# Attention turns: next rows' halves scaled by GpSimd and VectorE, one each, low parts behind; first exponential in front of the rows' high parts

## The reference

```python
gamma = (t @ gamma_w.T)[:, None, :]
beta = (t @ beta_w.T)[:, None, :]
return gamma * _rmsnorm(x) + beta
```

## Time and profile before

| | us |
|---|---|
| median of 3 runs | 1043.72 |
| lowest, highest | 1042.64, 1046.42 |
| profiled execution, its own time | 1053.19 |
| its span in the profile | 1051.4 |
| TensorE busy | 1021.5 (97%) |
| VectorE busy | 762.1 (72%) |
| ScalarE busy | 627.5 (60%) |
| GpSimd busy | 223.2 (21%) |

### The profile page before, as it was taken

How to read it: one execution, slowest core, us unless ns; L and a number is a source line. 1 busy time by engine, 2 the same in 40 slices (tenths; PEclk the granted TensorE clock), 3 DMA queues, 4 the chain that set the end, 5 groups by cost and what they waited for, 6 DMA issues and landing times.

```text
span 1051.4 us, 16503 instructions
## 1 busy us (share of the span) xinstructions
PE 1021.5 (97%) x5386; PEld 639.3 (61%) x5386; DVE 762.1 (72%) x1200; ACT 627.5 (60%) x850; POOL 223.2 (21%) x217
## 2 busy tenths in 40 slices
PE   7999999999999999999999999999999999999997
PEld 6776677778554344444444344443368788888885
DVE  5867668887767778778777877778955766667754
ACT  5455333352247777778777877777763545555455
POOL 1000001121122324333432333311202221212211
PEclk9999999999699999999999999999999999999999
DMA  9978644125424363553537354454220000000001
GB/s 288 379 189 241 160 109 115 31 41 151 104 63 154 79 192 68 165 124 104 149 77 207 73 163 101 133 137 105 72 61 21 1 21 21 20 20 0 21 21 41
DMA packets 92041, 110.95 MB, mean 106 GB/s; under 512 B 47184, under 2 KB 57424, under 8 KB 90960
## 3 DMA queue, kind: packets, MB, share of 16 engines
q1 hardware_dynamic: 60736, 100.56, 32.6%
q10 hardware_dynamic: 31248, 9.65, 5.3%
HBM read 65.81 MB, written 33.03 MB: 94 GB/s over the span
## 4 chain that ended last, share of the span: by engine, by line
PE 70%; DVE 9%; ACT 4%; issue 4%; DMA 3%; SPq 1%; ACTq 1%; POOL 1%; DVEq 0%; POOLq 0%
PE st_ps L1787 16%; PE st_ps L1639 9%; PE mx_ps L1787 8%; PE av_ps L1616 7%; PE val_ps L1491 6%; PE gate_ps L1491 5%; DVE mx L1202 5%; PE misc_ps L1547 3%; PE misc_ps L1663 3%; PE mx_ps L1571 3%; PE misc_ps L1676 2%; PE y_ps L1501 2%; DMA hf<-reciprocals 2%; DVE stage L1214 1%; PE misc_ps L1667 1%
## 5 line engine op out<-in xcount | busy, mean ns | idle before, releaser
L1202 DVE TENSOR_REDUCE mx<-mx_ps 128x1 f32<-128x512 f32 x488 | 313.4, 683 | 100.1 <-PE mx_ps L1571 97.8
L1571 PE MATMUL mx_ps<-kring,qring 48*128 48x512 f32 x500 | 198.4, 462 | 2.4 <-DVE mx L1202 1.5
L1639 PE MATMUL st_ps<-qring,kring 50*128 50x512 f32 x512 | 187.0, 445 | 4.7 <-ACT shared L928 4.6
L1639 PEld LDWEIGHTS st_ps<-qring,kring 50*128 50x128 f32 x512 | 76.3, 185 | 148.2 <-issue 112.7
L928 ACT ACTIVATE pbuf<-st_ps 128x1024 f32<-128x1024 f32 x128 | 129.4, 1023 | 41.8 <-PE st_ps L1639 40.4
L928 ACT ACTIVATE shared<-st_ps 128x1024 f32<-128x1024 f32 x128 | 128.0, 1022 | 38.0 <-PE st_ps L1639 37.1
L1571 PEld LDWEIGHTS mx_ps<-kring,qring 48*128 48x128 f32 x500 | 85.4, 185 | 24.9 <-DVE mx L1202 19.1
L1049 ACT ACTIVATE p_hi<-shared 128x512 fp32r<-128x512 f32 x64 | 40.4, 632 | 90.8 <-DVE shared L1382 88.6
L1387 DVE TENSOR_TENSOR p_lo<-shared,p_hi 128x512 fp32r<-128x512 f32 x64 | 52.3, 817 | 46.9 <-ACT p_hi L1049 46.9
L1382 DVE TENSOR_TENSOR shared<-st_ps,shared 128x512 f32<-128x512 f32 x64 | 43.9, 687 | 51.6 <-PE st_ps L1787 24.2
L1268 DVE SCALAR_TENSOR_TENSOR h<-val_ps,r,gelu 128x1024 f32<-128x1024 f32 x32 | 41.0, 1282 | 47.9 <-PE val_ps L1491 47.9
(11 more groups left out here) (241 smaller groups left out, 2103.9 us busy)
## 6 DMA issues: line engine op xcount, KB each, us to landing
chunk<-in_gen_w SPq DMA_DIRECT2D x8, 2048.0 KB, 9.2
qring<-q_parts SPq DMA_DIRECT2D x64, 192.0 KB, 3.5
kring<-k_parts SPq DMA_DIRECT2D x64, 192.0 KB, 4.6
q_parts<-stage SPq DMA_DIRECT2D x16, 512.0 KB, 2.9
k_parts<-stage SPq DMA_DIRECT2D x16, 512.0 KB, 2.8
xres<-in_xT SPq DMA_DIRECT2D x8, 512.0 KB, 11.4
shared<-in_x SPq DMA_DIRECT2D x8, 512.0 KB, 12.5
q_parts<-stage SPq DMA_DIRECT2D x16, 256.0 KB, 3.0
```

Of the source, the lines that this page charges most:

```text
L1202: nc.vector.tensor_reduce(mx[h // GH % 2][:, col:col + 1], mx_ps[:, qt % 2], AX, ALU.max).then_inc(S["mx_free"], 1)
L1571: nc.tensor.matmul(out, qring[h // GH][r:r + QROWS, h % GH // 2, qt * P:(qt + 1) * P], kring[h // GH][r:r + QROWS, h % GH // 2, :], start= ...
L1639: ins = nc.tensor.matmul(st_ps[half][:, kt % 2], kring[g][r:r + SROWS, i % GH // 2, kt * P:(kt + 1) * P], qring[g][r:r + SROWS, i % GH // ...
```

## The change

Four edits, all in the attention turns:

1. ScalarE, i = 0 of turns 2 to 7: the first of the step's two exponentials stands in front of the two high parts, and the second behind them.
2. GpSimd, same place: scales half 0 of `hf` when the first high part is there. Then it makes both low parts; for half 0 it waits for its own scaling, for half 1 for VectorE's.
3. VectorE, same place: scales half 1 alone, and waits for both high parts and for GpSimd's scaling of half 0 (`h` counts the halves in order).
4. GpSimd's turns 3 to 6 are written out instead of looped.

```diff
@@ gpsimd, step @@
                     for k in range(KD):
-                        wait(pool, "h" if rows_by_two(j) else "h_hi", KD * p + k + 1)
+                        wait(pool, "h_hi", KD * p + k + 1)
+                        if rows_by_two(j) and k == 0:
+                            nc.gpsimd.tensor_scalar(hf[:, k], hf[:, k], cv[:, C_GA, k, bass.ds(p, 1)],
+                                                    cv[:, C_BA, k, bass.ds(p, 1)], ALU.mult, ALU.add) \
+                                .then_inc(S["h"], 1)
+                        if rows_by_two(j):
+                            wait(pool, "h", KD * p + k + 1)
                         sub(m_lo[:, k], hf[:, k], m_hi[:, k].bitcast(F32)).then_inc(S["h_lo"], 1)
...
-            for turn in iterations(pool):
+            for j in range(1, NB + 1):
                 for i in range(NH):
-                    step(*turn, i)
+                    step(*flags(j), i)
@@ scalar, step @@
-                if i == 0 and has_p and rows_by_two(j):
-                    for k in range(KD):
-                        wait(act, "t", KD * p + k + 1)
-                        nc.scalar.activation(m_hi[:, k], hf[:, k], ACT.Identity,
-                                             scale=cv[:, C_GA, k, bass.ds(p, 1)],
-                                             bias=cv[:, C_BA, k, bass.ds(p, 1)]).then_inc(S["h_hi"], 1)
-                elif i == 0 and has_p and not opens:
+                if i == 0 and has_p and not opens and not rows_by_two(j):
                     scale_rows()
...
                         nc.scalar.activation(pbuf[g % 2][:, i % GH, 2 * half:2 * half + 2], st_ps[half][:],
                                              ACT.Exp, scale=float(DH) ** -0.5).then_inc(S["exp"], 1)
+                        if half == 0 and i == 0 and has_p and rows_by_two(j):
+                            for k in range(KD):
+                                wait(act, "t", KD * p + k + 1)
+                                nc.scalar.activation(m_hi[:, k], hf[:, k], ACT.Identity,
+                                                     scale=cv[:, C_GA, k, bass.ds(p, 1)],
+                                                     bias=cv[:, C_BA, k, bass.ds(p, 1)]).then_inc(S["h_hi"], 1)
@@ vector, step @@
                 if i == 0 and has_p and rows_by_two(j):
-                    for k in range(KD):
-                        wait(dve, "h_hi", KD * p + k + 1)
-                        nc.vector.tensor_scalar(hf[:, k], hf[:, k], cv[:, C_GA, k, bass.ds(p, 1)],
-                                                cv[:, C_BA, k, bass.ds(p, 1)], ALU.mult, ALU.add) \
-                            .then_inc(S["h"], 1)
+                    wait(dve, "h_hi", KD * (p + 1))
+                    wait(dve, "h", KD * p + 1)
+                    nc.vector.tensor_scalar(hf[:, 1], hf[:, 1], cv[:, C_GA, 1, bass.ds(p, 1)],
+                                            cv[:, C_BA, 1, bass.ds(p, 1)], ALU.mult, ALU.add).then_inc(S["h"], 1)
```

## The result

| | before | changed |
|---|---|---|
| median, us (20 runs each, one chip) | 1045.24 | 1049.56 |
| lowest and highest, us | 1042.64, 1053.51 | 1047.22, 1054.77 |
| profiled execution: own time, span, us | 1053.19, 1051.4 | 1048.26, 1046.5 |
| its mean granted clock | 0.987 | 0.998 |

The ratio is 1.0036, with a 95% interval of 1.0022 to 1.0051: **3.8 us slower** (2.3 to 5.3), inside the 0.5% that was called no change, and measurably above zero. The two profiled executions stand the other way round, by 4.9 us, and the one of before has the lower clock. They are compared by seams, in stretches where the clock is 1.00 in both, and not by their spans.

What follows compares the result with a forecast made beforehand. TensorE bounds the kernel; the seam depends on the early exponential and, more strongly, VectorE's return to its maxima. Four seams losing 4.0 us and two gaining 0.7 give +3.3 on 1043.72: 1047.0 us, range 1041.8 to 1050.0.

Steps and rivals of the forecast that it cites:

- seams: The six passages between two attention turns, into turns 2 to 7; 3 to 6 looped, 2 and 7 written out.
- likeliest class: Whole kernel: a change of under 5.2 us (about 0.5%) either way, which counts as no change; chance 0.73.
- B: Rival: VectorE's scaling is held by GpSimd's subtraction in all six seams; +5.6 us, 1049.3; chance 0.10.
- the forecast, held in four: VectorE held in turns 3 to 6, 4.0 us lost; free in 2 and 7, 0.7 gained; +3.3; chance 0.55.
- Exponential first: Step 1's start: up to 0.43 us gained a seam, 2.6 over six, only if VectorE is not later.
- the 5.12: Turn 4's first query product, us from t = 0 (ScalarE starting the high parts), said to be set by VectorE's maxima.
- GpSimd scales half 0: GpSimd at the seam: scaling starts at 1.80 behind the first high part and ends at 2.64.
- T: Duration of GpSimd's new scaling of half 0: taken as 0.84 us, between 0.62 and 1.28.
- Held in turns 3 to 6: Looped seams: GpSimd's subtraction starts first and VectorE's scaling is held; 1.00 us lost each, four times 4.0.
- So in turns 2 and 7 VectorE is first by some 0.05: Written-out seams: VectorE's scaling starts before GpSimd's subtraction; query product 4.99 against 5.32, 0.33 us gained, twice 0.7.
- Low parts: GpSimd's second subtraction, at most 2.5 us behind VectorE's scaling against 2.80 wanted: still covered by 0.3.
- the loop written out: GpSimd's turns 3 to 6: register operations lie in its 39 us of idle time per turn; zero cost.

Runs made afterwards that it cites:

- E alone: Kernel before with one edit, the first exponential put in front of the two high parts: ratio 1.0003 (0.9975 to 1.0031).
- own-semaphore run: Changed kernel, but VectorE's scaling of half 1 counts on a separate semaphore and no longer waits for GpSimd's scaling: ratio 1.0018 (0.9996 to 1.0041).
- S: Part of the change: half 0 scaled on GpSimd. Tried in the changed kernel with the high parts back in front of the exponential: ratio 1.0012.
- the better order: Changed kernel, but GpSimd scales each half before its subtraction, VectorE none; ScalarE runs high part 0, exponential, high part 1, exponential: ratios 0.9959, 0.9969.
- the run with VectorE written out: Changed kernel with a separate semaphore for VectorE's scaling of half 1, and VectorE's turns 3 to 6 written out: ratio 0.9988 (0.9958 to 1.0017).

## Why the prediction was right, and where it was not

The time was right: +3.3 us forecast, +3.8 measured (2.3 to 5.3), in the range, and within 0.5% as the likeliest class. The mechanism was right in the four looped turns and wrong in the two others. Of the cases on record it was B, held in all six, that came about; it had a chance of 0.10, and the forecast, held in four, had 0.55. By the seams the four looped turns cost 0.6 less than forecast and the two others 2.1 more, so the seams sum to 4.8 and not to 3.3. That the forecast stands 0.5 from the measured time is in part luck: one error partly covers the other, and the timing says less than the seams.

*Exponential first.* Right: TensorE's wait at step 1 went, and the gain was not taken, since VectorE was later. That the maxima and not the exponential set the 5.12 is shown by E alone (query product at 5.17, with TensorE free of the exponential). "Up to 0.43 a seam" was no gain at all by itself.

*GpSimd scales half 0.* T was taken as 0.84, from bounds of 0.62 and 1.28, and is 0.77. The 769 ns that the Trainium skill (GPSIMD Engine Reference, 3.1) has for such a loop over 512 elements is the measured median to the nanosecond. The start at 1.80 was 1.83.

*Held in turns 3 to 6.* Right, with its reason: GpSimd 0.08 behind its scaling, VectorE 0.19 to 0.21, of which 0.10 is the address operation. The working had "0.03 + 0.10 or more". The forecast with T at 0.77 gives a first maximum at 4.33 and a query product at 6.05, and 4.29 and 6.02 were measured. It was forecast at 1.00 lost for each of these seams, and is 0.80 to 0.90; over four that is 3.4 in place of 4.0.

*"So in turns 2 and 7 VectorE is first by some 0.05"*: this step failed. The 0.03 came from a ScalarE row. VectorE behind GpSimd takes 0.11 (353.84 to 353.95) and 0.12, with no address operation in between, so GpSimd's 0.08 beats it. Forecast: 0.33 gained at each, 0.7 in all; in fact 0.70 lost at each, 1.4 in all. Rival B had this mechanism, and the price that it gave, +5.6, is 0.8 over the seams' 4.8, since T was 0.07 and the hold 0.06 shorter than the forecast took them, six times each.

*And being first by 0.05 may not have been enough.* The own-semaphore run has VectorE's record 0.05 to 0.07 ahead of GpSimd's in turns 3 to 6, and VectorE is held in all four. The Trainium skill (SBUF — State Buffer, "Who interferes with whom") gives the shared port pair to whoever issues first. The records of 1.44 to 1.63 for 0.54 agree with it; by the starts of the records alone, these four would speak against it. So a lead of up to 0.07 us by the starts of the records did not tell who gets the pair, and one of 0.13 or more did. All four lost seams are looped and all won ones are written out, so no run here separates the size of the lead from the computed address.

*Low parts, the loop written out.* Both at nothing, and right: the low product still follows by 1.04 (1.03 before), and the loop alone gives 1.0007.

*Not seen in the prediction:* that the loss is an interaction. E and S were costed one after the other and then summed, and no line asked what S costs without E. The loss needs GpSimd's subtraction to begin (2.68) just as VectorE is done with its maxima (2.49), and it is E's 0.92 that puts it there.

What stays open: the seams sum to 4.8 and the timings say 3.8 and 4.3. Their intervals hold 4.8. From t = 0 of turn 2 to t = 0 of turn 7, a stretch with five seams that sum to 4.1, the traces give 301.94 us before and 305.51 and 305.37 in the two profiles of the changed kernel: 3.4 to 3.6 more. So most of the loss stays. Whether the rest is given back later in a turn is not shown, since single turns of one profile differ by 1.0 us in length (59.99 and 60.97 before).

## What to carry to other kernels

When two engines hold each other up and both are released by the same event, decide the order with a semaphore. One changed wait in front of GpSimd's subtraction took away the whole loss, where start latencies of 0.03 to 0.1 us taken from other rows named the wrong winner in two seams of six. Take a start latency from a row with the same pair of engines, in the same kind of code (looped or written out).

And ask of a stage that is moved not only what it costs, but what it lands on. Here the exponential's move and the split of the scaling were each free alone; the better order gave the long chain on the idle engine its input first (the first high part), and then the exponential that TensorE waits for.

## What was not expected of the hardware

- VectorE lost the race although its record began 0.05 to 0.07 us ahead of GpSimd's (four looped seams), and won at 0.13 to 0.23 ahead (eight written-out seams in two kernels). Where it lost, its record was 1.61 to 1.63 for 0.54.
- VectorE's scaling was not held by GpSimd's *scaling*: in the run with VectorE written out it begins 0.14 before that one's end in turn 4 (473.60, and 472.96 + 0.78) and takes 0.55. It begins there within the last 0.25 of GpSimd's record, so whether an earlier start would be held is not shown.
- A held VectorE scaling ends 0.29 after the subtraction's end (477.24 against 476.95), that is, it gets going 0.25 before that end; in phase A it was 0.19.
- GpSimd's scaling with two pointer operands costs 767 to 771 ns for 512 columns in the changed kernel (758 to 779 over all kernels here), 60% of its two-input subtraction (1.28). VectorE's takes 0.54.
